# A graph layer on one core: edge loop with compared row numbers, a fully split second layer, powers on GpSimd, and routing in steps

## What is computed

```
h   = layernorm(x)
# message of each edge (i = src, j = dst, w = edge weight)
m   = silu([h_i, h_j, w] @ mW1 + mb1)             # 513 -> 256
m   = silu(layernorm(m, g, b) @ mW2 + mb2)        # 256 -> 256
agg = segment_sum(m, src, 3125)
gnn = h + silu([h, agg] @ uW1 + ub1) @ uW2 + ub2
x   = x + gnn + mix(h)          # mix: linear attention, 8 heads
# router and experts: top 2 of 8, softmax weights, 256 -> 512 (exact gelu) -> 256
x   = x + experts(layernorm(x))
```

## Time and profile before

| what | value |
|---|---|
| runs | 1616.96, 1613.83, 1616.63 us |
| the profiled execution | 1614.69 us, its span 1612.9 us |
| PE busy over the span | 1431.6 us (89%) |
| DVE | 1186.1 us (74%) |
| ACT | 981.2 us (61%) |
| POOL | 839.8 us (52%) |
| mean granted clock of PE | 0.933 |

### The profile page before, as it was taken

One profiled execution on the slowest core, in us unless ns is written; L12 is line 12 of the kernel. 1 busy time (PEld: TensorE's weight loads), 2 busy tenths in 40 slices (PEclk: granted clock), 3 DMA queues, 4 the chain that ended last, 5 costly groups with the idle time before them and its releaser, 6 DMA issues.

```text
span 1612.9 us, 34882 instructions
## 1 busy us (share of the span) xinstructions
PE 1431.6 (89%) x8790; PEld 1183.5 (73%) x8791; DVE 1186.1 (74%) x4460; ACT 981.2 (61%) x2146; POOL 839.8 (52%) x1203
## 2 busy tenths in 40 slices
PE   4565999979899999999999999999998945999991
PEld 2454665556799999999999999998996633777771
DVE  7999436652899999989999999989993466444442
ACT  1342224431688888888888888888884252666560
POOL 1487750014366666666666666666640002666651
PEclk7655999989799999999999999999999977999996
DMA  7400120001122222222222222222733062444437
GB/s 193 90 4 5 46 59 1 1 23 56 40 75 73 74 73 72 73 73 74 72 72 72 74 73 73 74 72 72 73 66 138 1 230 83 66 68 65 71 56 255
DMA packets 63010, 118.03 MB, mean 73 GB/s; under 512 B 21729, under 2 KB 41473, under 8 KB 62450
## 3 DMA queue, kind: packets, MB, share of 16 engines
q0 software_dynamic: 36560, 77.33, 20.7%
q1 hardware_dynamic: 25616, 36.80, 7.2%
q10 hardware_dynamic: 780, 3.24, 0.5%
HBM read 92.57 MB, written 24.72 MB: 73 GB/s over the span
## 4 chain that ended last, share of the span: by engine, by line
PE 78%; DVE 13%; ACT 4%; issue 3%; DMA 2%; DVEq 0%; ACTq 0%; POOLq 0%
PE ps L937 13%; PE ps L692 9%; PE ps L1029 6%; PE ps L917 6%; PE ps L907 5%; PE ps L824 5%; PE ps L904 4%; PE ps L899 4%; PE ps L900 4%; PE ps L788 3%; DVE place_val_t L1392 3%; PE ps L927 2%; DVE lane_hot_e_t L1387 2%; PE ps L1056 2%; PE ps L1055 2%
## 5 line engine op out<-in xcount | busy, mean ns | idle before, releaser
L640 POOL DMA_INDIRECT msg_t<-dst_table,stage_idx x448 | 446.9, 998 | 107.6 <-issue 46.3
L937 PE MATMUL ps<-msg_t,hot_t 128*125 128x256 f32 x896 | 241.5, 392 | 13.7 <-issue 7.4
L1160 ACT ACTIVATE msg1n_t<-msg_t,nw_b,nw_y 128x256 f32<-128x256 f32 x448 | 243.7, 598 | 0.0
L1177 ACT ACTIVATE msg_t<-msg_t 128x512 f32<-128x512 f32 x224 | 141.5, 632 | 100.9 <-DVE msg_t L1572 100.8
L899 PE MATMUL ps<-w_hi_t,msg1T_hi_t 128*128 128x256 f32 x672 | 198.5, 310 | 0.0
L606 POOL DMA_INDIRECT sorted_edges<-sort_sb_t,chunk_to x112 | 136.0, 1214 | 86.2 <-DVE chunk_to L1379 52.7
L900 PE MATMUL ps<-w_lo_t,msg1T_hi_t 128*128 128x256 f32 x672 | 179.8, 282 | 0.0
L937 PEld LDWEIGHTS ps<-msg_t,hot_t 128*125 128x125 f32 x896 | 151.2, 188 | 31.8 <-issue 9.6
L917 PE MATMUL ps<-src_hi_t,hotT_t 127*128 x448 | 160.8, 379 | 3.7 <-ACT hotT_t L1173 3.7
L1572 DVE TENSOR_TENSOR msg_t<-ps,msg_t 128x512 f32<-128x512 f32 x224 | 152.5, 681 | 3.4 <-PE ps L917 3.4
L904 PE MATMUL ps<-w_hi_t,msg1T_lo_t 128*128 128x256 f32 x672 | 153.6, 283 | 0.0
(11 more groups left out here) (346 smaller groups left out, 3569.5 us busy)
## 6 DMA issues: line engine op xcount, KB each, us to landing
w_sb_t<-in_L_ffn_W_dram SPq DMA_DIRECT2D x16, 512.0 KB, 7.9
msg_t<-dst_table,stage_idx POOLq DMA_INDIRECT x448, 2.8
res_t<-in_x_dram SPq DMA_DIRECT2D x1, 3125.0 KB
total<-zero_chunks_t SPq DMA_DIRECT2D x1, 3125.0 KB, 39.4
dst_table<-dst_stage SPq DMA_DIRECT2D x25, 125.0 KB
xm_table<-xm_t POOLq DMA_DIRECT2D x5, 625.0 KB, 7.4
total<-res_t SPq DMA_DIRECT2D x1, 3125.0 KB
sum_b_t<-total ACTq DMA_DIRECT2D x5, 625.0 KB, 11.2
```

Of the source, the lines that this page charges most:

```text
L640: pool.indirect_dma_start(out=msg1[:, k, j, :], out_offset=None, in_=dst_table, in_offset=bass.IndirectOffsetOnAxis(stage_idx[:, half, q:q ...
L937: m = pe.matmul(bank(7, D, rows=NP), hot[:, (k - 8) % TURN, j, 0:NP].bitcast(F32), msg2[:, k % 2, j, :], start=(j == 0), stop=(j == G - 1))
L1160: m = A(msg1n[:, (k + 1) % 2, j, :], msg1[:, kk, j, :], ACT.Identity, bias=nw_b[:, kk, j:j + 1], scale=nw_y[:, kk, j:j + 1])
L1177: A(v, v, ACT.Silu).then_inc(msg1_sb, 1)
```

## The change

In the edge loop:

- hotT is no longer transposed from hot. The row numbers of all edges and the weights (hi, lo) are written to DRAM once (row_list as fp16, weight_rows). SP loads them back for five units at a time: the row numbers spread over all partitions (near_rows, two buffers), the weights as the two last rows of hotT (ten slots). DVE compares the row numbers with the partition's own number and writes hotT, one step ahead. The comparison that makes hot stays and moves to the end of DVE's step for unit n - 7, into two slots.
- The second layer is split in all four pieces (fp32r; no fp32 matmul).
- The sums over edges go to two PSUM banks in turn, so PE waits for DVE's addition of one unit earlier.
- PE loads block numbers at k = 0, 4 and 7, all ahead of L917's group; DVE loads ten at once at k = 0.
- DVE gives variance + eps of a pair (nw_v), POOL makes the power -0.5 in one instruction, DVE makes the shift in two. POOL then issues the four gathers of a pair six units ahead. The fence and the weights' instruction are gone.
- Two trips of the hardware loop, 20 steps, are written out ahead instead of one.

Around it: the buffers of the update move from "work" to "weights"; in the update each chunk gets its own power on POOL, raw logits are copied from PSUM, maxima and index searches of a chunk follow two chunks later, and ACT writes xm of early blocks beside the update. The counts for the routing are made from the last column of a scan (8 columns instead of 400). PE waits for the remainders of the experts' second weights only at the first product that needs them. One DMA to totals is cut in two.

The core of the diff (renamed semaphores, buffer offsets and moved asserts are left out):

```diff
+sp.wait_ge(side_hi_ok, 2)
+sp.dma_start(row_list.rearrange("(g p e) -> p g e", g=LOADS, p=LT), side_rows[0:LT]).then_inc(side_out, 16)
+sp.wait_ge(side_lo_ok, 1)
+for v in range(2):
+    sp.dma_start(weight_rows[v].rearrange("(g p e) -> p g e", g=LOADS, p=LT), side_w[0:LT, v].bitcast(F32))\
+      .then_inc(side_out, 16)
+sp.wait_ge(side_out, 48)
+sp.wait_ge(w2_split, 1)
+for h, m in enumerate(range(0, UNITS, NEAR)):
+    some = min(NEAR, UNITS - m)
+    if h >= 2:
+        sp.wait_ge(hotT_sb, m - NEAR)
+    sp.dma_start(near_rows[h % 2][:, 0:some, :].rearrange("p k e -> p (k e)"),
+                 row_list[m * UE:(m + some) * UE].partition_broadcast(128)).then_inc(near_in[h % 2], 16)
+    if h >= 2:
+        sp.wait_ge(pre_ps, m - NEAR)
+    sp.dma_start(hotT[NP:HR, m % TURN:m % TURN + some, :].bitcast(F32),
+                 weight_rows[:, m * UE:(m + some) * UE].rearrange("v (k e) -> v k e", e=UE))\
+      .then_inc(weights_in[h % 2], 16)
...
+def roots(m, k, free):
+    pool.wait_ge(spread_ok, m // 2 + 1 if isinstance(m, int) else pairs + k // 2 + 1)
+    if not isinstance(free, int) or free > 0:
+        pool.wait_ge(msg1n_sb, free)
+    pool.tensor_tensor(nw_y[:, k:k + 2, :], nw_v[:], minus_half[:].rearrange("p (a b) -> p a b", b=G),
+                       ALU.pow).then_inc(pow_ok, 1)
+def stage(m, k, turn):
+    if k in PARTS:
+        some = min(PARTS[k], UNITS - m) if isinstance(m, int) else PARTS[k]
+        for q in range(k, k + some):
+            after(pool, row_in[q], 32 * turn)
+        st.did(pool.tensor_copy(stage_idx[:, G * k:G * (k + some)], recs[:, bass.ds(G * m, G * some), 0]))
+        st.join()
+def gather(k):
+    for j in range(G):
+        pool.indirect_dma_start(
+            out=msg1[:, k, j, :], out_offset=None, in_=dst_table,
+            in_offset=bass.IndirectOffsetOnAxis(stage_idx[:, G * k + j:G * k + j + 1], 0)).then_inc(row_in[k], 16)
+pairs = 0
+def edge_pair(m, k, i):
+    ahead, slot = m + AHEAD_UNITS, k + AHEAD_UNITS
+    if here(ahead, UNITS):
+        stage(ahead, slot % TURN, i + slot // TURN)
+    roots(m, k, ahead + 2 - TURN)
+    for q in range(2):
+        if here(ahead + q, UNITS):
+            gather((slot + q) % TURN)
...
         for j in range(G):
-            split = [c for c in range(KD) if c * UE + j * 128 < SPLIT]
-            for c in split:
+            for c in range(KD):
                 pe.matmul(o[j], part(msg1T_hi, j, c), w2_hi[:, c, :], start=(c == 0), stop=False)
                 pe.matmul(o[j], part(msg1T_hi, j, c), w2_lo[:, c, :], start=False, stop=False)
             if j == 0:
                 pe.wait_ge(msg1T_lo_sb, m_ + 1)
-            for c in split:
-                m = pe.matmul(o[j], part(msg1T_lo, j, c), w2_hi[:, c, :], start=False,
-                              stop=(c == KD - 1))
-            if len(split) < KD:
-                m = pe.matmul(o[j], msg1T_f[:, (k + 1) % 2, :], w2c[:, KD - 1, :], start=False, stop=True)
+            for c in range(KD):
+                m = pe.matmul(o[j], part(msg1T_lo, j, c), w2_hi[:, c, :], start=False, stop=(c == KD - 1))
         m.then_inc(msg2_ps, 1)
-    if k == 0:
-        load_blocks(mybir.EngineType.PE, blk, n, 0, 3)
+    if k in (0, 4, 7):
+        load_blocks(mybir.EngineType.PE, blk, n, k, 4 if k == 0 else 3)
     if here(n, UNITS):
-        after(pe, hotT_sb, n + 1)
+        pe.wait_ge(hotT_sb, n + 1)
+        if k % NEAR == 0:
+            pe.wait_ge(weights_in[k // NEAR], turn_weights)
         after(pe, pre_sb, n - 1)
         for j in range(G):
             for first, table in ((True, src_hi), (False, src_lo)):
-                m = pe.matmul(bank(1 + k % 2, D, first=j * D), hotT[0:HR, k % 2, j * 128:j * 128 + 128],
+                m = pe.matmul(bank(1 + k % 2, D, first=j * D), hotT[0:HR, k, j * 128:j * 128 + 128],
                               table[0:HR, bass.ts(blk[k], 1), :].rearrange("p a n -> p (a n)"),
                               start=first, stop=not first)
         m.then_inc(pre_ps, 1)
-    m_ = n + 1
-    if here(m_, UNITS):
-        pe.wait_ge(hot_ready, m_ + 1)
-        pe.wait_ge(hot_weight, m_ + 1)
-        after(pe, hotT_sb, m_)
-        for j in range(G):
-            m = pe.matmul(bank(0, 128, rows=HR, first=j * 128), hot[:, (k + 1) % TURN, j, 0:HR], ident_r[:],
-                          start=True, stop=True)
-        m.then_inc(hotT_ps, 1)
-    if k in (1, 5):
-        load_blocks(mybir.EngineType.PE, blk, n + 2, k + 2, 4 if k == 1 else 3)
-    m_ = n - 8
+    m_ = late - 8
     if here(m_, UNITS):
         pe.wait_ge(msg2_sb, m_ + 1)
-        after(pe, sum_sb, m_)
+        pe.wait_ge(hot_ready, m_ + 1)
+        after(pe, sum_sb, m_ - 1)
         for j in range(G):
-            m = pe.matmul(bank(7, D, rows=NP), hot[:, (k - 8) % TURN, j, 0:NP].bitcast(F32), msg2[:, k % 2, j, :],
+            m = pe.matmul(bank(7 * (kl % 2), D, rows=NP), hot[:, kl % 2, j, 0:NP], msg2[:, kl % 2, j, :],
                           start=(j == 0), stop=(j == G - 1))
         m.then_inc(sum_ps, 1)
-steps(pe, edge_step, -1, LAST, 1, UNITS // TURN - 1, TURN)
...
-        A(msg1T_hi[:, k % 2], bank(3 + k % 2, SPLIT), ACT.Copy)
-        A(msg1T_f[:, k % 2], bank(3 + k % 2, 128, first=SPLIT), ACT.Copy).then_inc(msg1T_sb, 1)
-    m_ = n - 5
-    kk = (k - 5) % TURN
+        A(msg1T_hi[:, kl % 2], bank(3 + kl % 2), ACT.Copy).then_inc(msg1T_sb, 1)
...
+def edge_step(n, k, turn_near, turn_rows):
     m_ = n + 1
     kk = (k + 1) % TURN
     if here(m_, UNITS):
-        after(dve, sum_ps, m_ - TURN + 1)
-        rows = recs[:, bass.ds(G * m_, G), 1:2]
-        dve.tensor_tensor(hot[:, kk, :, 0:NP], iota[:, 1:NP + 1].unsqueeze(1).broadcast_to([128, G, NP]),
-                          rows.broadcast_to([128, G, NP]), ALU.is_equal).then_inc(hot_ready, 1)
-    if k % 2:
-        rstd_step(0, slot, pair_on)
+        if kk % NEAR == 0:
+            dve.wait_ge(near_in[kk // NEAR], turn_near)
+        after(dve, pre_ps, m_ - TURN + 1)
+        dve.tensor_scalar(hotT[0:NP, kk, :], near_rows[kk // NEAR][0:NP, kk % NEAR, :], row_col[0:NP, :], None,
+                          ALU.is_equal).then_inc(hotT_sb, 1)
+    if k % 2 and here(n - 3, UNITS):
+        slot = (k - 3) % TURN
+        st.join()
+        dve.tensor_scalar(nw_v[:], emv[:, slot:slot + 2, :, 1], EPS, None, ALU.add).then_inc(spread_ok, 1)
+    m_ = n - 4
+    pair_on = k % 2 == 0 and here(m_, UNITS)
+    shifts = nw_b[:, (k - 4) % TURN // 2 * 2:(k - 4) % TURN // 2 * 2 + 2, :]
+    if pair_on:
+        slot = (k - 4) % TURN
+        dve.wait_ge(pow_ok, m_ // 2 + 1 if isinstance(m_, int) else pairs + (k - 4) // 2 + 1)
+        nw.did(dve.scalar_tensor_tensor(shifts, emv[:, slot:slot + 2, :, 0], -1.0, nw_y[:, slot:slot + 2, :],
+                                        ALU.mult, ALU.mult))
     if k == 0:
-        load_blocks(mybir.EngineType.DVE, blk, n - 9, 0, 4)
-    rstd_step(first_q, slot, pair_on)
+        load_blocks(mybir.EngineType.DVE, blk, n - 9, 0, TURN)
     m_ = n - 9
     if here(m_, UNITS):
         dve.wait_ge(sum_ps, m_ + 1)
         after(dve, sum_sb, m_)
         a = agg[0:NP, bass.ts(blk[k], 1), :].rearrange("p a n -> p (a n)")
-        dve.tensor_tensor(a, a, bank(7, D, rows=NP), ALU.add).then_inc(sum_sb, 1)
-    rstd_step(first_q + 1, slot, pair_on)
-    if here(n - 6, UNITS):
-        dve.wait_ge(msg1T_sb, n - 5)
-        after(dve, msg2_ps, n - 7)
-        dve.tensor_tensor(msg1T_lo[:, k % 2], bank(3 + k % 2, SPLIT),
-                          msg1T_hi[:, k % 2].bitcast(F32), ALU.subtract)\
+        dve.tensor_tensor(a, a, bank(7 * ((k + 1) % 2), D, rows=NP), ALU.add).then_inc(sum_sb, 1)
+    if pair_on:
+        nw.join()
+        dve.tensor_scalar(shifts, shifts, 1.0, None, ALU.add).then_inc(rstd_ok, 1)
+    m_ = n - 6
+    if here(m_, UNITS):
+        dve.wait_ge(msg1T_sb, m_ + 1)
+        after(dve, msg2_ps, m_ - 1)
+        dve.tensor_tensor(msg1T_lo[:, k % 2], bank(3 + k % 2), msg1T_hi[:, k % 2].bitcast(F32), ALU.subtract)\
            .then_inc(msg1T_lo_sb, 1)
-    rstd_step(first_q + 2, slot, pair_on)
     m_ = n - 1
     kk = (k - 1) % TURN
     if here(m_, UNITS):
         dve.wait_ge(msg1_sb, m_ + 1)
-        st.did(dve.bn_stats(est[:, kk, 0, :], msg1[:, kk, 0, :]))
-    rstd_step(first_q + 3, slot, pair_on)
-    if here(m_, UNITS):
-        st.did(dve.bn_stats(est[:, kk, 1, :], msg1[:, kk, 1, :]))
-    rstd_step(first_q + 4, slot, pair_on)
+        for j in range(G):
+            st.did(dve.bn_stats(est[:, kk, j, :], msg1[:, kk, j, :]))
     if here(n, UNITS):
         dve.wait_ge(pre_ps, n + 1)
         dve.wait_ge(row_in[k], turn_rows)
...
         dve.tensor_tensor(v, bank(1 + k % 2), v, ALU.add).then_inc(pre_sb, 1)
     if here(m_, UNITS):
         st.join()
-    rstd_step(first_q + 5, slot, pair_on)
+    m_ = n - 7
+    if here(m_, UNITS):
+        after(dve, sum_ps, m_ - 1)
+        rows = recs[:, bass.ds(G * m_, G), 1:2]
```

(47 more changed lines are left out.)

322 lines of the change are left out of this document (136 added, 186 removed).

## The result

| | before | after |
|---|---|---|
| time, median (lowest to highest) | 1616.45 us (1613.83 to 1616.96, 4 runs) | 1551.49 us (1549.81 to 1554.71, 4 runs) |
| profiled execution, its span | 1614.69, 1612.9 | 1554.71, 1553.0 |
| one turn of the edge loop (10 units) | 36.08 | 33.46 |

The ratio is 0.9604, with an interval of 0.9585 to 0.9622: faster by 65 us, where 82.5 were forecast (1532, range 1509 to 1568). That holds for the chip on which both were timed. I call this another chip; the record has numbers for the chips of the experiments alone, and the time of the kernel before is what tells them from the result's. So there are two questions: why 65 and not 82.5 us, and why the sign differs there.

The account below looks back on a forecast made before the run. TensorE bounds the loop, VectorE 0.14 below; after the change they are level at 3.21 and 3.29. Taking 3.29: loop -71, start +2, routing -13.5, so 1614.69 - 82.5 = 1532 us; own range 1520 to 1548, whole 1509 to 1568.

Parts of the forecast that it names:

- case C: Edge loop: the round between ScalarE and VectorE and register stalls add up, 3.43 a unit, 1563 us; chance 17%.
- One sign: Edge loop: VectorE busier than TensorE, above 95%, with TensorE at 96 to 98% of its shorter step.
- TensorE, 3.51 to 3.21 a unit: Edge loop: transposes and an fp32 matmul go, three fp32r matmuls come, -0.30 a unit.
- case D: Edge loop: TensorE keeps its packed pace, 3.21 a unit, and routing is at its better end: 1509 us; chance 14%.
- VectorE, 3.29: Edge loop: VectorE's need per unit falls from 3.37 to 3.29 us, register load included, bounds 3.1 and 3.45.
- The three register loads a turn become one of ten numbers: Edge loop, VectorE: one load near the step's start replaces three, adding 0.08 us a unit.
- The power: Edge loop, GpSimd: one power over 128x4 per pair of units takes 0.5 us, bounds 0.2 and 1.2, and is hidden.
- case B: Edge loop: VectorE's comparison and GpSimd's gathers exclude each other; mean hold 0.6 a unit, 1666 us; chance 4%.
- Gathers six units ahead, 0: Edge loop, GpSimd: gathers six units ahead instead of up to ten, asked for 9.9 us before use, cost 0.
- Start +2: Ahead of the edge loop: first row-number transfers and 20 written-out steps cost +2 us together, bounds -1 and +6.
- Routing -13.5: Behind the loop: earlier maxima and searches, powers, smaller counts and later expert-weight remainders give -13.5 us, bounds -6 and -18.
- Raw logits ... each fits beside it: 0: Update: row copies on ScalarE, raw logits and powers fit beside TensorE's chain and cost 0, at worst +3 us.

Follow-up runs that it names:

- gathers_half_loads: Kernel after, with one of two gathers per unit from the second turn and VectorE's register loads as 1, 3, 3, 3: 1598.0 us, ratio 0.9466.
- all_three: Kernel after, with register loads as 1, 3, 3, 3, the second weight's split made earlier and the logits copy moved ahead: 1717.5 us, ratio 1.0167.

## Why the prediction was right on its chip, and where its terms were off

The direction and the mechanism were right there: TensorE's step shrank as forecast, and VectorE, level with it, took part of that back. But 1551 lies outside the 1520 to 1548 that I gave the forecast itself; it is in the range only because the range reaches over case C, whose cause was another, and in that sense the hit is luck. The loop, the start, the update and the routing were all off to the same side. One sign failed too: VectorE was not busier than TensorE, 93% against 98%.

- *TensorE, 3.51 to 3.21 a unit:* right to the hundredth, and so is the 1.0 us of stalls at its own register loads, which went. `gathers_half_loads` reaches the packed 32.13 a turn that I had as case D.
- *VectorE, 3.29:* the parts were near (comparison forecast 0.30, 0.352 with its tail; behind the stall one addition to agg follows the other at 843.87 and 846.92, 3.05 apart). The step that failed is "The three register loads a turn become one of ten numbers. The first ... is the visible stall of 0.8 us now ... and the new one stands there too": I priced a load by its place and not by its count. It stalls 2.10, not 0.8. Of the surplus over the room that the other engines leave, 1.35 a turn comes through. The turn was 33.46 for the 32.9 forecast, the loop -60.8 for -71. This is shown in the kernel with half the gathers, where the loads spread give 32.13 for 33.48 and the waits are those of the result; on the chip of the result it was not run. The Trainium skill, Runtime: NRT & Kernel Launch, section "Instruction fetch mechanics", gives some 200 ns per register for such a load; the traces agree, with 0.22.
- *ScalarE's round (case C):* its time of 1563 is nearer to 1551 than the forecast's 1532, but only because start, update and routing came out worse than forecast; in the loop 3.345 a unit is nearer to the forecast's 3.29 than to its 3.43. Its cause is out: with the load spread nothing of the round is left.
- *The power:* 1.04 us, not 0.5, within the bounds. Hidden on the chip of the result (GpSimd waits 25.9 us for VectorE there), but GpSimd then needs 6.27 of the 6.69 us of a pair.
- *Exclusion of VectorE and GpSimd (case B):* 352 ns mean for the comparison, next to the 346 of the earlier trace rows. Between 440 and 1150 us 188 comparisons ran beside a gather, with a median of 0.333 us and a longest of 0.508, and 25 with GpSimd idle, with a median of 0.321: no hold. The rule of the Trainium skill (SBUF — State Buffer, "Who interferes with whom"), as I applied it to the issuing of gathers, is not borne out by these.
- *Gathers six units ahead, 0:* right on the chip of the result. On the others the gathers are what turns the gain into a loss (half of them gone, 0.961 for 1.027), and the 0 is wrong there. No run gives their lead of six units a part in it; that they stand four in a row is what the traces speak for, and it was not tested alone. I had looked at their distance and count, and never at what issuing them does to other engines.
- *Start +2:* +7.65. The transfer of row numbers cost 2.15, as forecast. 5.5 came ahead of it, in code that the change leaves alone: 2.0 up to 345 us, and then two groups of matmuls took 3.45 and 5.51 where the same took 1.76 and 3.74 before, at a granted clock of 0.61 against 0.83 between 350 and 360 us. It stood at the lower level from 344.2 to 357.9 us, where before it did so from 342.9 to 346.3 and from 356.5 to 363.3; why was not tested.
- *Routing -13.5:* -10.4. The first part, up to the lists of slots, gave -5.4 where the terms add up to -8.5: the counts and passes gave the -3.8 forecast and a little more (-4.2), but maxima, searches and roots -1.2 for -4.7, since three copies of raw logits, a power of 1.02 us and nine each of the maxima and searches still stand behind the update. The rest, with the remainders out of the way, -5.0, as forecast. "Raw logits ... each fits beside it: 0" failed: TensorE's logits matmul now waits for the copy of the block before, queued on VectorE behind the 1.26 us of additions, 0.68 us in each of five chunks. That is the update's +3.35; moving the copy took it away in `all_three`.

What stays open: why the result and the experiments differ (the chip, or something else that changed between them: all four numbered chips were alike, and neither kernel was timed again where the kernel before takes 1616), what holds the rise back, and whether bursts of two with the rest of the change would keep the gain everywhere. GpSimd has 0.4 us a pair to spare at that pace, so pauses would cost time; it was not tried. On the chips of the experiments no complete version beat the kernel before; `all_three` comes nearest, at 1.017, and was not run on the chip of the result.

## What to carry to other kernels

A register load costs by its numbers: before batching loads, compare the longest one with the room that the engine has at that point, since two loads that fit are cheaper than one that doesn't. When the engines are level, ask of each term how far it comes in one piece, not only how much it is per turn. A gain in a loop where all engines are level should be measured on more than one chip before it is believed. And a probe that takes half of something away changes its number as well as its order: to blame the order, keep the number.

## What the hardware showed that I had not expected

- The same two kernels stand at a ratio of 0.960 on one chip and of 1.027 on another: the turn of the kernel after is 33.46 and 39.2 us, while that of the kernel before is 36.1 in both places.
- There, in a burst of four gathers (4.8 us), TensorE's semaphores rise up to 2.2 us late (median), most of them together, 5.5 to 6.0 us from its start; in a burst of two they come by about 2.9 us. VectorE's stay at 0.01 in the median, and so do ScalarE's where they are recorded. During the train of scatters ahead of the loop, VectorE's small instructions without a wait start 0.7 or 1.4 us apart instead of 0.07.
- Adding 1.04 us of work for each pair to the 64%-busy GpSimd did not slow the kernel there: 1.0201 of before against 1.0272 for the unaltered kernel in the next group, with intervals that just touch.
